# A fused attention and feed-forward layer: the newest head's counts first in ScalarE's step, layer norm in one pass per tile, feed-forward products taken out of PSUM by VectorE

## What is computed

```
x = x + layernorm(attn(layernorm(x)))
x = x + layernorm(ffn(layernorm(x)))

attn:  dots = einsum(q, k) * scale;  dots = einsum('bhij,hk->bkij', dots, pre_proj)
       dots = where(causal, -max, dots)
       vk = top_k(dots, 64)[..., -1:];  dots = where(dots < vk, -max, dots)
       p = softmax(dots);  p = einsum('bhij,hk->bkij', p, post_proj);  out = (p @ v) @ Wo + bo
ffn:   h = silu(x @ wg.T) * (x @ wu.T);  out = h @ wd.T          (128 -> 384 -> 128)
layernorm(x) = (x - mean) / sqrt(var + 1e-5)
```

## Time and profile before

| | |
|---|---|
| Median of 3 runs | 3607.39 us (3606.74 to 3607.62) |
| The profiled execution: own time, span | 3610.26 us, 3608.5 us |
| Granted TensorE clock, mean | 0.881 |
| Busy: TensorE, VectorE, ScalarE, GpSimd | 2833.9, 2962.0, 3177.0, 2009.9 us |

### The profile page before, as it was taken

One profiled execution on the slowest core, in us unless ns is written; L12 is line 12 of the kernel. 1 busy time (PEld: TensorE's weight loads), 2 busy tenths in 40 slices (PEclk: granted clock), 3 DMA queues, 4 the chain that ended last, 5 costly groups with the idle time before them and its releaser, 6 DMA issues. The chain is left out here.

```text
span 3608.5 us, 70619 instructions
## 1 busy us (share of the span) xinstructions
PE 2833.9 (79%) x13751; PEld 1830.1 (51%) x13751; DVE 2962.0 (82%) x12236; ACT 3177.0 (88%) x9018; POOL 2009.9 (56%) x3687
## 2 busy tenths in 40 slices
PE   7788787878868887788878768877787888777765
PEld 3455555555545555555555545555455555555544
DVE  4588888888888888888888888888888888888883
ACT  1799999999979999999999979998899999999982
POOL 3355655555555565655655545564655555565544
PEclk9888989898988988888998988988898898989876
DMA  1000000000000000000000000000000000000000
GB/s 41 7 2 2 5 8 5 8 2 5 8 4 8 5 2 8 5 8 5 8 2 5 8 4 8 5 8 2 5 8 5 8 5 2 8 5 8 2 7 4
DMA packets 31403, 22.65 MB, mean 6 GB/s; under 512 B 3201, under 2 KB 30338, under 8 KB 30722
## 3 DMA queue, kind: packets, MB, share of 16 engines
q1 hardware_dynamic: 30722, 16.03, 1.6%
HBM read 11.83 MB, written 4.19 MB: 4 GB/s over the span
## 5 line engine op out<-in xcount | busy, mean ns | idle before, releaser
L881 ACT ACTIVATE signs<-scores,state 128x528 int8<-128x528 f32 (+3 forms) x3072 | 1760.0, 573 | 199.5 <-DVE state L1102 106.6
L1276 POOL TENSOR_SCALAR probs<-probs,rinv 128x528 f32<-128x528 f32 (+3 forms) x1024 | 541.4, 549 | 1416.3 <-DVE rinv L1132 1415.3
L747 PE MATMUL t_bank<-ident,probs 128*128 128x128 f32 x2560 | 519.4, 329 | 590.1 <-POOL probs L1276 540.8
L1284 POOL TENSOR_TENSOR work<-scores,work 128x528 f32<-128x528 f32 (+3 forms) x1024 | 887.6, 903 | 15.8 <-DVE work L1024 15.8
L723 PE MATMUL s_bank<-xn,gT 128*128 128x512 f32 (+3 forms) x2048 | 800.0, 515 | 9.5 <-ACT gT L813 6.8
L734 PEld LDWEIGHTS y_bank<-u_all,probsT 128*128 128x128 f32 x5120 | 631.3, 197 | 135.5 <-issue 122.6
L747 PEld LDWEIGHTS t_bank<-ident,probs 128*128 128x128 f32 x2560 | 312.0, 160 | 712.3 <-issue 554.9
L734 PE MATMUL y_bank<-u_all,probsT 128*128 128x128 f32 x5120 | 636.9, 281 | 7.8 <-ACT probsT L892 7.7
L1127 DVE SCALAR_TENSOR_TENSOR probs<-scores,kth,expo 128x528 f32<-128x528 f32 (+3 forms) x1024 | 521.9, 564 | 82.4 <-issue 70.9
L881 ACT ACTIVATION_READ_ACCUMULATOR signs<-scores,state 128x1 f32 x3072 | 573.8, 187 | 0.0
L1024 DVE TENSOR_SCALAR_CACHE_REDUCE work<-scores,state 128x528 f32<-128x528 f32 (+3 forms) x1024 | 527.6, 553 | 46.6 <-DVE state L1102 41.4
(11 more groups left out here) (148 smaller groups left out, 3240.2 us busy)
## 6 DMA issues: line engine op xcount, KB each, us to landing
xwork<-in_L_attn_x_dram SPq DMA_DIRECT2D x17, 256.0 KB, 2.9
xres<-in_L_attn_x_dram SPq DMA_DIRECT2D x16, 256.0 KB, 3.0
out_dram<-ybuf SPq DMA_DIRECT2D x16, 256.0 KB, 2.4
u_all<-in_L_attn_Wq_dram SPq DMA_DIRECT2D x1, 512.0 KB, 3.8
u_all<-in_L_attn_Wk_dram SPq DMA_DIRECT2D x1, 512.0 KB, 4.6
u_all<-in_L_attn_Wv_dram SPq DMA_DIRECT2D x1, 512.0 KB, 5.4
u_all<-in_L_attn_Wo_dram SPq DMA_DIRECT2D x1, 512.0 KB
expo<-in_L_ffn_w_gate_dram SPq DMA_DIRECT2D x1, 192.0 KB, 4.8
```

The lines of the kernel that those rows point to most:

```text
L747: mm = nc.tensor.transpose(t_bank[q % 2][:, at:at + P], probs[:, h % 2, KEY_AT[t] + j * P:KEY_AT[t] + (j + 1) * P], ident[:, :])
L881: nc.scalar.activation(signs[:, k, 0:ROW[t]], row(scores, ring(head_of(s, k + 1), RING), t), ACT.Sign, bias=guesses(s % STATES, k, GUESSES ...
L1276: nc.gpsimd.tensor_scalar(prb, prb, rinv[:, slot_p, t:t + 1], 1.0, ALU.mult, ALU.mult).then_inc(scaled, 1)
L1284: nc.gpsimd.tensor_tensor(wrk, row(scores, slot_k, t), wrk, ALU.subtract).then_inc(hidden, 1)
```

## The change

- ScalarE's step becomes count(0), count(2), (`ybuf`), count(1), first extra, turned(0), G, flags, turned(1), exponential 0, turned(2), second extra, exponentials 1 to 3. `counts` gets two halves, by the parity of the step.
- `f_gate` is no longer copied (and its name serves only the set-up), and UP is not copied by ScalarE. In steps 10 to 12 (one earlier than before) VectorE forms (1 + tanh) * gate with the gate read from its PSUM bank, waits till that is written and UP(c) is made, and multiplies by UP(c) out of PSUM. These two free the banks. GpSimd's product and the semaphores `silu_pool`, `silu_ready` go.
- `norm` on GpSimd: after the power, four instructions of 128 x 128 that subtract the mean and multiply by the inverse deviation at once. `ln_out` counts to 4 per norm.
- `misc_free` becomes one semaphore per bank; a use waits for the earlier uses of its own bank (`turns_of_bank`). Where one wait stood for two copies (`memory_y`, the memory maxima, the statistics of Z) two stand now.

```diff
@@ ScalarE, take_extra @@
                         elif use[0] == "GATE":
 
-                            act.wait_ge(silu_ready, HC * (b - 1) + 1)
                             act.wait_ge(misc_full, misc_index(kind, b, use) + 1)
-                            nc.scalar.activation(f_tanh[:, use[1], :], misc[misc_place(kind, par, use)][:, :], ACT.Tanh, scale=0.5)
-                            nc.scalar.copy(f_gate[:, use[1], :], misc[misc_place(kind, par, use)][:, :]).then_inc(misc_free, 1)
+                            nc.scalar.activation(f_tanh[:, use[1], :], misc[misc_place(kind, par, use)][:, :], ACT.Tanh,
+                                                 scale=0.5).then_inc(tanh_ready, 1)
                         elif use[0] == "UP":
-                            take(kind, b, par, use, f_up[:, use[1], :])
+                            pass
@@ ScalarE, count @@
-                                                 accum_out=counts[:, k * T + t:k * T + t + 1]
+                                                 accum_out=counts[:, s % 2, k * T + t:k * T + t + 1]
@@ ScalarE, step @@
+                    count(0)
                     count(2)
...
                     take_turned(1)
-                    count(0)
+                    exponentials(0)
+                    take_turned(2)
                     take_extra(1)
-                    take_turned(2)
-                    for p in range(T):
+                    for p in range(1, T):
                         exponentials(p)
@@ VectorE, step @@
-                    if 11 <= s < 11 + HC and kind != "first":
-
-                        c = s - 11
-                        dve.wait_ge(silu_pool, HC * (b - 1) + c + 1)
+                    if 10 <= s < 10 + HC and kind != "first":
+
+                        c = s - 10
+                        gate_at, up_at = misc_place(kind, par, ("GATE", c)), misc_place(kind, par, ("UP", c))
+                        dve.wait_ge(tanh_ready, HC * (b - 1) + c + 1)
+                        alone(dve)
                         v.scalar_tensor_tensor(out=f_up[:, c, :], in0=f_tanh[:, c, :], scalar=1.0,
-                                               in1=f_up[:, c, :], op0=ALU.add, op1=ALU.mult).then_inc(silu_ready, 1)
+                                               in1=misc[gate_at][:, :], op0=ALU.add, op1=ALU.mult
+                                               ).then_inc(misc_free[gate_at], 1)
+                        dve.wait_ge(misc_free[gate_at], turns_of_bank(kind, b, misc_at(kind, ("GATE", c))) + 1)
+                        dve.wait_ge(misc_full, misc_index(kind, b, ("UP", c)) + 1)
+                        alone(dve)
+                        v.tensor_tensor(f_up[:, c, :], f_up[:, c, :], misc[up_at][:, :], ALU.mult).then_inc(misc_free[up_at], 1)
...
-                        v.tensor_tensor(miss, counts[:, :], aim_sum, ALU.subtract).then_inc(guess_step, 1)
+                        v.tensor_tensor(miss, counts[:, (s - 1) % 2, :], aim_sum, ALU.subtract).then_inc(guess_step, 1)
@@ GpSimd, norm @@
-                nc.gpsimd.tensor_tensor(dst[:, :, :], src[:, :, :], meanvar[:, :, 0:1].to_broadcast([P, T, D]),
-                                        ALU.subtract).then_inc(ln_centred, 1)
-                pool.wait_ge(ln_centred, n + 1)
-                alone(pool)
-                nc.gpsimd.tensor_tensor(dst[:, :, :], dst[:, :, :], rstd[:, :].unsqueeze(2).to_broadcast([P, T, D]),
-                                        ALU.mult).then_inc(ln_out, 1)
+                for t in range(T):
+                    nc.gpsimd.tensor_scalar(dst[:, t, :], src[:, t, :], meanvar[:, t, 0:1], rstd[:, t:t + 1], ALU.subtract,
+                                            ALU.mult).then_inc(ln_out, 1)
@@ GpSimd, extras @@
-                    if 10 <= s < 10 + HC:
-                        c = s - 10
-                        pool.wait_ge(misc_free, misc_index(kind, b, ("UP", c)) + 1)
-                        alone(pool)
-                        nc.gpsimd.tensor_tensor(f_up[:, c, :], f_up[:, c, :], f_gate[:, c, :], ALU.mult).then_inc(silu_pool, 1)
@@ TensorE, share: a use waits for the earlier uses of its own bank @@
-                at_least(pe, misc_free, misc_index(kind, b, use) - 1)
+                n = misc_at(kind, use)
+                at_least(pe, misc_free[n % 2], turns_of_bank(kind, b, n))
```

More of the change, by code:

```diff
@@ L191, with misc_first @@
 PLACE = {k: {u: i for i, u in enumerate(USES[k])} for k in KINDS}
-def misc_index(kind, b, use):
+MISC_BATCH = len(USES["mid"])
+assert MISC_BATCH % 2 == 0
+def misc_first(kind):
     n = 0 if kind == "pro" else len(USES["pro"])
@@ L198, in misc_index, with misc_at, turns_of_bank, from_last @@
         n += len(USES["first"])
-    if kind == "mid":
-        n = (b - 1) * len(USES["mid"]) + n
     if kind in ("last", "drain"):
-        n += len(USES["mid"]) * (B - 2)
+        n += MISC_BATCH * (B - 2)
     if kind == "drain":
         n += len(USES["last"])
-    return n + PLACE[kind][use]
+    return n
+def misc_at(kind, use):
+    return misc_first(kind) + PLACE[kind][use]
+def misc_index(kind, b, use):
+    return misc_at(kind, use) + ((b - 1) * MISC_BATCH if kind == "mid" else 0)
 def misc_place(kind, par, use):
-    b = {"pro": 0, "first": 0, "mid": 2 - par, "last": B - 1, "drain": B}[kind]
-    return misc_index(kind, b, use) % 2
-def from_last(kind, b, use):
+    return misc_at(kind, use) % 2
+def turns_of_bank(kind, b, n):
+    return n // 2 + ((b - 1) * (MISC_BATCH // 2) if kind == "mid" else 0)
+def from_last(kind, use):
     back = {len(USES[k]) - PLACE[k][use] for k in {"mid": ("first", "mid"), "last": ("mid",), "drain": ("last",)}[kind]}
     assert len(back) == 1
-    return misc_index(kind, b, USES[kind][0]) - back.pop()
-def g_index(kind, b, s):
+    return misc_first(kind) - back.pop()
+def g_at(kind, s):
     if s > 0:
-        return misc_index(kind, b, ("G", s))
+        return misc_at(kind, ("G", s))
     if kind == "first":
-        return misc_index("pro", 0, ("G", H))
-    return from_last(kind, b, ("G", H))
-def flag_index(kind, b, s):
+        return misc_at("pro", ("G", H))
+    return from_last(kind, ("G", H))
+def flag_at(kind, s):
     if s > 0:
-        return misc_index(kind, b, ("FLAG", s - 1))
-    return from_last(kind, b, ("FLAG", H - 1))
+        return misc_at(kind, ("FLAG", s - 1))
+    return from_last(kind, ("FLAG", H - 1))
 def ln_index(kind, b, what):
@@ L326, in build @@
         state = sb("state", [P, 2 * (STATES - 1) * STATE + PART])
-        counts = sb("counts", [P, GUESSES * T])
+        counts = sb("counts", [P, 2, GUESSES * T])
         between = sb("between", [P, 2, GUESSES * T])
@@ L413, in build @@
         misc_full = sem("misc_full")
-        misc_free = sem("misc_free")
+        misc_free = [sem(f"misc_free{i}") for i in range(2)]
+        tanh_ready = sem("tanh_ready")
         scores_full = sem("scores_full")
@@ L466, in keys, with freed @@
             return tensor[:, bass.ds(slot, 1), KEY_AT[t]:KEY_AT[t] + KEYS[t]].squeeze(1)
+        def freed(engine, kind, b, n):
+            engine.wait_ge(misc_free[n % 2], turns_of_bank(kind, b, n) + 1)
         def mem_parts(flat):
@@ L706, in memory_y @@
             def memory_y(kind, b):
-                pe.wait_ge(misc_free, misc_index(kind, b, ("PM", 1)) + 1)
+                for i in range(2):
+                    freed(pe, kind, b, misc_at(kind, ("PM", i)))
                 for t in range(T):
@@ L812, in take @@
                 act.wait_ge(misc_full, misc_index(kind, b, use) + 1)
-                nc.scalar.copy(dst, misc[misc_place(kind, par, use)][:, :] if src is None else src).then_inc(misc_free, 1)
+                nc.scalar.copy(dst, misc[misc_place(kind, par, use)][:, :] if src is None else src).then_inc(
+                    misc_free[misc_place(kind, par, use)], 1)
             def take_values(kind, b, par, u):
@@ L981, in memory_maxima @@
             def memory_maxima(kind, b, par):
-                dve.wait_ge(misc_free, misc_index(kind, b, ("MEM", 1)) + 1)
+                for half in range(2):
+                    freed(dve, kind, b, misc_at(kind, ("MEM", half)))
                 at_least(dve, masked, 4 * H * b)
@@ L1160, in step @@
                     if s == 15 and kind != "first":
-                        dve.wait_ge(misc_free, misc_index(kind, b, ("DOWN", 1)) + 1)
+                        for i in range(2):
+                            freed(dve, kind, b, misc_at(kind, ("DOWN", i)))
                         norm_stats(kind, b, "Z", ybuf)
@@ L1195, in norm @@
                 alone(pool)
[L1196 to L1201 removed]
+                for t in range(T):
+                    nc.gpsimd.tensor_scalar(dst[:, t, :], src[:, t, :], meanvar[:, t, 0:1], rstd[:, t:t + 1], ALU.subtract,
+                                            ALU.mult).then_inc(ln_out, 1)
             def add_residual(kind, b, what, dst, done):
[L1204 removed]
+                pool.wait_ge(ln_out, 4 * ln_index(kind, b, what) + 4)
                 alone(pool)
@@ L1217, in _ @@
```

(2 more changed lines are left out.)

25 lines of the change are left out of this document (10 added, 15 removed).

## The result

| | before | after |
|---|---|---|
| Median | 3607.1 us (3604.9 to 3607.6) | 3651.9 us (3640.8 to 3658.4) |
| Ratio, 95% interval | | 1.0122 [1.0097, 1.0148] |
| Profiled execution: own time, span | 3610.3, 3608.5 us | 3650.8, 3649.0 us |
| Granted TensorE clock, mean | 0.881 | 0.878 |

A forecast was written before the change was run, and what follows sets the result against it. ScalarE, busy 88% of the span, and its waits were taken as the bound. Terms -3.9 - 2.8 + 8.75 - 0.4 + 3.55 = +5.2 us a batch, +78 over 15, -5 at the ends: 3680 us, range 3575 to 3740.

The forecast's parts named there:

- UP ahead of the moves: Steps 10 to 12: VectorE's second product waits for UP with the moves queued behind; ScalarE waits 3.15, 2.8, 2.8: +8.75 a batch.
- waits for the moves at 0, 2, 8, 9, 13: ScalarE's waits for VectorE's moves shrink: -3.9 us a batch at steps 0, 2, 8, 9, and -0.4 at step 13.
- six copies less on ScalarE: Three f_up and three f_gate copies of 0.47 us leave ScalarE: -2.8 us a batch.
- the second extra: ScalarE waits for TensorE at the extra's earlier copy, up to 0.8 at steps 0, 3, 12, 13, 14: +3.55 a batch.
- The order: count(0) ahead of count(2) in ScalarE's step: 0.65 us more slack for the moves; the flag becomes VectorE's next late wait.
- The norms: Four GpSimd instructions of 0.35 replace two of 1.04; shorter holds take 0.6 us off each of four move chains a batch.
- The bound of 5.5 for this term: The largest gain allowed from slack and shorter holds at steps 0, 2, 8 and 9: -5.5 us a batch.
- the mark: The start of count(2) in a step, which opened ScalarE's step before the change; the forecast's times are counted from it.
- Rival 1: UP is there in time or VectorE's wait is hidden: -3.6 us a batch, 3548 us; chance 0.13.
- Rivals 2 and 3: 2: TensorE's clock stays high, 3572 us, chance 0.1. 3: holds don't shrink, chain matmuls all slow, 3720 to 3750, 0.14.
- Rival 4: The edits don't do what they say and other mixtures cancel: within 0.2% of before; chance 0.05.

The follow-up runs named there:

- e2: The kernel before with only the one-pass norm (four GpSimd instructions per norm): 3577.5 us, ratio 0.9913.
- e6: The changed kernel with the second extra moved behind exponential 2 instead of behind turned(2): 3627.1 us, ratio 1.0051 to the kernel before.
- e7: The changed kernel with the edits of both e5 and e6: 3515.3 us, ratio 0.9734 to the kernel before.
- e9: e7 with the norm as eight GpSimd instructions of one pointer each, four subtracting and four multiplying: 3597.7 us, ratio 0.9984 to the kernel before.
- e5: The changed kernel with VectorE's second product, by UP(c), moved behind the moves and rinv of the same step: 3555.3 us, ratio 0.9855 to the kernel before.
- e8: The changed kernel with the two-pass norm put back: 3708.5 us, ratio 1.0277 to the kernel before.
- F: The feed-forward products out of PSUM; alone (changed kernel with old order and old norm): 3683.9 us, ratio 1.0210 to the kernel before.
- N: The norm in one pass; alone on the kernel before: 3577.5 us, ratio 0.9913.

## Why the prediction was right

The sign and the main mechanism, UP ahead of the moves, held; the time was 28 us below the forecast. Per batch (measured: in the batch read above):

| term | predicted | measured |
|---|---|---|
| waits for the moves at 0, 2, 8, 9, 13 | -3.9 - 0.4 | -8.0 |
| six copies less on ScalarE | -2.8 | -2.8 |
| UP ahead of the moves, steps 9 to 11 | +8.75 | +8.25 |
| the second extra | +3.55 | +5.3 |
| sum | +5.2 | +2.8 (the windows: +3.3) |

**The order** did what it said: VectorE's third MAX8 now waits for the flag (11.1 us in eight waits in the batch above), and ordinary steps are 12.06 and 12.55 long.

**The norms** are the term that failed. "I take 0.35 each, 1.4 in place of 2.2" took its price from the earlier trace rows, where one operand is a pointer and the other a constant; with two pointers it is 0.79, and 1.08 to 1.53 beside VectorE's masked probabilities: a norm in the batches takes 3.1 to 4.0. That the new instructions are short was thus false. And "with shorter POOL instructions each hold is shorter" named the right gain for the wrong reason: the pieces are longer than thought and hold hardly at all. So all of the 8.0 went and not half of it, and the wait at step 0, which was to be 1.5 to 2, is gone. (8.0 is this batch; the whole run had 106.6, some 7.1 a batch.) The wrong price did little harm in this kernel (ScalarE waits 101.4 us for `probsT` over the whole run, 93.4 before); in e2, e6, e7 and e9, where other waits had gone, it came out. The bound of 5.5 for this term was too narrow, since it counted on some hold.

**The copies** cost what was taken: a step with one extra less is 0.48 to 0.49 shorter, and both products last 688 ns. But ScalarE's busy time was to fall by 45 and fell by 26.8. It is idle 299 times for over 0.15 us in the run, 141 times before, and an instruction behind a wait doesn't overlap with the one ahead: by estimate 158 times 0.1, some 16 us, count as busy in place of the overlap.

**UP ahead of the moves**: steps 9, 10 and 11 last 45.05 us (14.08, 14.98, 15.99). The forecast had 15.75 + 15.0 + 15.0 = 45.75 (its waits of 2.8 are 2.9 by its own numbers, 15.0 less 12.1, which would put it 3 us higher). The chain was right in each link; turn 2 stood 6.43, 6.59 and 6.56 behind the mark (6.44 and 6.2 assumed), and the passes to UP's end were 5.08, 5.81 and 6.86, where the forecast's sums give 6.75 (it read 6.91 and doesn't say why it took less), 6.2 and 6.2. The slow one came last and not first, as TensorE's clock went: 1.00, 0.81 and 0.69 in the three passes. Of the 8.25 ScalarE spends only 5.5 at the marks; 2.1 are its waits for `f_tanh` and the flags in the same steps. e5, which removes the queue and nothing else, is 97 us faster. Rival 1 needed these waits under 3.6 and is out.

**The second extra** waits 0.76 at a time, as said (0.8), but at seven steps and not at five: 0, 1, 8, 12, 13, 14 and 15. Steps 8 and 15 were left out because they "wait for VectorE anyway", and that wait was the one that vanished; step 3, which was counted in, hardly waits in this batch. 4.7 us, and each wait costs 0.1 more than it shows (below).

**Rivals 2 and 3.** Both kinds of pass occur, so neither a high clock nor a low one throughout. Holds that don't shrink, half of rival 3, are what e8 has: 3708.5, just under the 3720 to 3750 given for both halves. Rival 4, within 0.2% of before, is out at 1.2%. The Trainium skill (Perfetto Trace Analysis, Identifying Performance Opportunities) would have improvement come from the most-contended engine. F took 2.8 us a batch from ScalarE, and alone it cost 77 us: an engine that is 88% busy still ends its steps by what it waits for.

The forecast lay 28 us high, and 32 for the profiled execution (3683 against 3650.8): 1.9 for the batch read, 2.2 by the mean of the middle batches (+5.2 against +3.0). Behind it are errors of both signs, -3.7 for the moves, -0.5 for UP and +1.75 for the extra. That the second large one offset half of the first is luck; the sign didn't need it, since the sum with the moves alone put right is still +1.5. The 0.5 a batch between the sum of the terms and the window stands in steps 0 and 3, as waits too short for the view: in step 0 the flag copy starts 0.69 behind G (0.48 undisturbed) and turned(0) 0.53 behind the extra (0.47), in step 3 the U copy starts 0.47 behind turned(2) (0.26). Still open is why GpSimd's instruction is slow: the number of its pointers explains only a part (e9).

## What to carry to other kernels

Where every engine takes its list in order, ask of each wait that a change adds what stands behind it in the queue, and put the wait behind whatever others need soonest: one product moved behind the eleven moves was worth 97 us without a single instruction less. Price a part together with the rest, since parts that remove the same waits don't add up (50 - 29 + 77 gave 45). And when the last wait of a stretch goes, look up which waits it had covered: they are the next bill.

## What the runs showed of the hardware

- GpSimd's tensor_scalar on 128 x 128 float32 with two pointer operands takes 0.79 us, and 1.08 and 1.34 beside VectorE's masked probabilities; with one pointer some 0.60; with one pointer and a constant, 144 columns take 0.39. Two tensor_tensor passes over 512 columns (2.08) are faster than four of the first kind (3.13).
- That instruction hardly holds VectorE's operations with two SBUF inputs (0.16 to 0.18 each inside it in the stretch of e2, none of 438 over 0.39 in after), while a tensor_tensor of 1.04 to 1.26 us holds a 0.17 us subtraction for 0.95 and 1.18. The slower form was thus the better one for this kernel: N alone gives 29 us, and in the changed kernel it is worth 57.
- A wait on ScalarE costs about 0.1 us more than the profile's idle time: a step of 12.55 with one wait of 0.76 lasts 13.41. Neighbours overlap by some 0.1 us elsewhere, and the instruction behind a wait doesn't overlap with the one ahead of it.
- TensorE's passes from turn 2 to UP took 5.08 us at a granted clock of 1.00, 5.81 at 0.81 and 6.86 at 0.69; the two slower ones came behind 3.98 and 3.96 us of idle time.
